# Layer-norm statistics of the output blocks taken by two accumulating passes on ScalarE in place of bn_stats on VectorE

## The reference, cut to what matters

```python
# x: (8, 2048, 1024) f32; 8 routed experts, top 2 of them weighted, and one shared expert; I = 1408
x = x + _layernorm(local_attention(_layernorm(x), w1, w2, v))       # window of 16 tokens
x = x + _layernorm(moe(_layernorm(x), w_router, wg, wu, wd, wg_s, wu_s, wd_s))

def _layernorm(x, axis=-1, eps=1e-5):
    m = jnp.mean(x, axis=axis, keepdims=True)
    v = jnp.var(x, axis=axis, keepdims=True)
    return (x - m) / jnp.sqrt(v + eps)
```

## Time and profile before

| what | us |
|---|---|
| median of 3 runs | 3217.65 |
| the profiled execution, its time | 3216.99 |
| its span (slowest core, core 4) | 3215.3 |
| spans of the 8 cores | 3204.2 to 3215.3 |
| last block's addition into osc ends | 3212.3 |

### The profile page before, as it was taken

How to read it: one execution, slowest core, us unless ns; L and a number is a source line. 1 busy time by engine, 2 the same in 40 slices (tenths; PEclk the granted TensorE clock), 3 DMA queues, 4 the chain that set the end, 5 groups by cost and what they waited for, 6 DMA issues and landing times.

```text
span 3215.3 us, 31801 instructions; the slowest of 8 cores (3204.2 to 3215.3 us)
## 1 busy us (share of the span) xinstructions
PE 2517.7 (78%) x11570; PEld 1123.4 (35%) x11570; DVE 1210.1 (38%) x2366; ACT 527.0 (16%) x474; POOL 506.6 (16%) x550
## 2 busy tenths in 40 slices
PE   2654554542128999999999999689999999999995
PEld 0221121210013444444444444334444444444442
DVE  5564655656543222222222222532222222222225
ACT  2422517061211011001001001010010010010010
POOL 0000000000002122222222222122222222222220
PEclk9986877766558999999999999799999999999997
DMA  7000000000206679669679777577787778878773
GB/s 165 1 0 1 1 1 1 1 0 0 20 1 64 63 66 91 62 64 91 66 66 85 71 74 72 81 79 67 65 86 72 71 74 75 76 66 79 75 65 73
DMA packets 626055, 179.41 MB, mean 56 GB/s; under 512 B 618608, under 2 KB 619760, under 8 KB 625904
## 3 DMA queue, kind: packets, MB, share of 16 engines
q0 software_dynamic: 621344, 160.55, 53.2%
q1 hardware_dynamic: 4560, 16.84, 1.5%
HBM read 329.48 MB, written 8.39 MB: 105 GB/s over the span
## 4 chain that ended last, share of the span: by engine, by line
PE 71%; DVE 14%; ACT 8%; issue 3%; DMA 2%; DVEq 2%; ACTq 0%; SPq 0%; POOLq 0%
PE py L944 21%; PE pg L856 12%; PE pu L871 12%; PE py L871 10%; PE py L856 10%; ACT tanb L394 6%; DVE uwide L470 3%; PE pq L320 2%; PE pq L339 1%; DVEq L62 1%; DVE bnb L154 1%; DVE argb L388 1%; DMA x<-x 1%; PE psc L403 1%; DMA wdb<-wd 1%
## 5 line engine op out<-in xcount | busy, mean ns | idle before, releaser
L944 PE MATMUL py<-hpr,wdb 128*128 128x512 bf16 x3168 | 706.3, 385 | 48.2 <-DVE hpr L893 40.0
L944 PEld LDWEIGHTS py<-hpr,wdb 128*128 128x128 bf16 x3168 | 312.0, 99 | 436.3 <-issue 81.0
L856 PE MATMUL pg<-xm_fm,wgb 128*128 128x512 bf16 x1728 | 394.9, 382 | 3.0 <-DVE cwb L811 3.0
L871 PE MATMUL pu<-xm_fm,wub 128*128 128x512 bf16 x1728 | 390.6, 379 | 0.0
L842 POOL DMA_DIRECT2D wgb<-wg x176 | 156.4, 889 | 1455.4 <-DVE x L577 812.3
L962 DVE SCALAR_TENSOR_TENSOR yfm<-py,yfm 128x1024 f32<-128x1024 f32 x128 | 156.8, 1225 | 487.3 <-PE py L944 480.3
L885 DVE TENSOR_TENSOR t1b<-sgb,pu 128x1024 bf16<-128x1024 bf16 x108 | 131.9, 1221 | 527.0 <-PE pu L871 527.0
L871 PE MATMUL py<-xm_fm,wub 128*128 128x512 bf16 x1440 | 325.5, 379 | 0.0
L856 PE MATMUL py<-xm_fm,wgb 128*128 128x512 bf16 x1440 | 325.5, 379 | 0.0
L881 ACT ACTIVATE sgb<-pg 128x1024 bf16<-128x1024 f32 x108 | 110.6, 1024 | 1297.6 <-PE pg L856 1297.6
L403 PE MATMUL psc<-tanb,vspb 128*16 128x512 bf16 x512 | 154.6, 431 | 188.6 <-ACT tanb L394 188.5
(11 more groups left out here) (119 smaller groups left out, 1308.6 us busy)
## 6 DMA issues: line engine op xcount, KB each, us to landing
wgb<-wg POOLq DMA_DIRECT2D x176, 256.0 KB, 5.2
wub<-wu POOLq DMA_DIRECT2D x176, 256.0 KB, 5.4
wdb<-wd POOLq DMA_DIRECT2D x128, 352.0 KB, 6.8
x<-x SPq DMA_DIRECT2D x4, 2048.0 KB, 27.7
out<-osc SPq DMA_DIRECT2D x16, 512.0 KB, 2.6
wgb<-wgs POOLq DMA_DIRECT2D x22, 256.0 KB, 5.3
wub<-wus POOLq DMA_DIRECT2D x22, 256.0 KB, 5.8
wdb<-wds POOLq DMA_DIRECT2D x16, 352.0 KB, 6.6
```

Of the source, the lines that this page charges most:

```text
L856: last = e.matmul(gb[:, gg * 512:(gg + 1) * 512], wgb[sl][:, c * 128:(c + 1) * 128], xm_fm[:, c * T + tof + gg * 512: c * T + tof + (gg + ...
L871: last = e.matmul(ub[:, gg * 512:(gg + 1) * 512], wub[sl][:, c * 128:(c + 1) * 128], xm_fm[:, c * T + tof + gg * 512: c * T + tof + (gg + ...
L944: last = e.matmul(pbank[pyn][:, gg * 512:(gg + 1) * 512], wdb[sl][:, ic * 128:(ic + 1) * 128], hpr[:, ic * TH + gg * 512: ic * TH + (gg + ...
```

## The change

The `bn_stats` and `bn_aggr` instructions of the epilogue go. In their place ACT reads the PSUM tile twice: an Identity activation that writes the block to `ytv` and accumulates the sum over the row, and a Square activation that writes to `osc` (the result is overwritten later in the same block) and accumulates the sum of squares. Four small DVE instructions make the mean and the variance of these two sums. The normalisation (L1015 before, L1027 after) reads `ytv` and no longer PSUM. The PSUM tile is given back to PE by the Square pass. The wait for `ytv_chain` moves from the normalisation on DVE to the Identity pass on ACT, and the Square pass gets the wait for the output DMA of two blocks before.

```diff
-                    for gi in range((H + 511) // 512):
...
-                        P.add("vector", lambda e, gi=gi, s0_=s0_, wdt=wdt, ob=ob,
-                              blk=blk: e.bn_stats(
...
-                    P.add("vector", lambda e, po=po, blk=blk: e.bn_aggr(
-                        agg2[:, po: po + 2],
-                        bnb[:, (blk % 2) * 12: (blk % 2) * 12 + 6 * nst]))
+                    zi = blk % 2
+                    evs1 = P.add("scalar", lambda e, ob=ob, zi=zi, po=po:
+                                 e.activation(
+                        ytv[zi][:], ob[:, 0:H], AF.Identity,
+                        accum_out=agg2[:, po: po + 1]),
+                        waits=[ev_yt, ytv_chain[0]], inc="s")
+                    evs2 = P.add("scalar", lambda e, ob=ob, zi=zi, po=po:
+                                 e.activation(
+                        osc[zi][:], ob[:, 0:H], AF.Square,
+                        accum_out=agg2[:, po + 1: po + 2]),
+                        waits=[evs1] + ev_out_dma[-2:-1], inc="s")
+                    free_ev[obk] = evs2
+                    P.add("vector", lambda e, po=po: e.tensor_scalar(
+                        agg2[:, po: po + 1], agg2[:, po: po + 1], 1.0 / H, None,
+                        op0=A.mult), waits=[evs2])
+                    P.drain("vector")
+                    P.add("vector", lambda e, po=po: e.tensor_scalar(
+                        agg2[:, po + 2: po + 3], agg2[:, po: po + 1],
+                        agg2[:, po: po + 1], None, op0=A.mult))
+                    P.drain("vector")
+                    P.add("vector", lambda e, po=po: e.tensor_scalar(
+                        agg2[:, po + 1: po + 2], agg2[:, po + 1: po + 2], 1.0 / H,
+                        None, op0=A.mult))
+                    P.drain("vector")
+                    P.add("vector", lambda e, po=po: e.tensor_tensor(
+                        agg2[:, po + 2: po + 3], agg2[:, po + 1: po + 2],
+                        agg2[:, po + 2: po + 3], op=A.subtract))
                     P.drain("vector")
                     evv = P.add("vector", lambda e, po=po: e.tensor_scalar(
-                        agg2[:, po + 2: po + 3], agg2[:, po + 1: po + 2], EPS,
+                        agg2[:, po + 2: po + 3], agg2[:, po + 2: po + 3], EPS,
                         None, op0=A.add), inc="v")
...
-                    evz = P.add("vector", lambda e, zi=zi, po=po, ob=ob:
-                                e.tensor_scalar(
-                        ytv[zi][:], ob[:, 0:H], agg2[:, po: po + 1],
+                    evz = P.add("vector", lambda e, zi=zi, po=po: e.tensor_scalar(
+                        ytv[zi][:], ytv[zi][:], agg2[:, po: po + 1],
                         agg2[:, po + 3: po + 4], op0=A.subtract, op1=A.mult),
-                        waits=[ev_a4, ytv_chain[0]], inc="v")
-                    free_ev[obk] = evz
+                        waits=[ev_a4], inc="v")
```

More of the change, by code:

```diff
@@ L987, in build_program @@
                     po = 4 * (blk % 2)
-                    for gi in range((H + 511) // 512):
-                        s0_ = gi * 512
-                        wdt = min(512, H - s0_)
-                        P.add("vector", lambda e, gi=gi, s0_=s0_, wdt=wdt, ob=ob,
-                              blk=blk: e.bn_stats(
[L993 to L997, removed]
@@ L1012, in build_program @@
                     P.drain("vector")
-                    zi = blk % 2
-                    evz = P.add("vector", lambda e, zi=zi, po=po, ob=ob:
-                                e.tensor_scalar(
-                        ytv[zi][:], ob[:, 0:H], agg2[:, po: po + 1],
+                    evz = P.add("vector", lambda e, zi=zi, po=po: e.tensor_scalar(
+                        ytv[zi][:], ytv[zi][:], agg2[:, po: po + 1],
                         agg2[:, po + 3: po + 4], op0=A.subtract, op1=A.mult),
-                        waits=[ev_a4, ytv_chain[0]], inc="v")
-                    free_ev[obk] = evz
+                        waits=[ev_a4], inc="v")
                     P.drain("vector")
```

## The result

The changed kernel takes 3235.42 us in the median, against 3218.21 for the kernel before measured beside it: the ratio is 1.0058, with a 95% interval of 1.004 to 1.0077. A second set of runs gave 1.0045 (1.0027 to 1.0063). It is a little slower, by about 16 us. The rows after come from the profile of the second set (span 3231.7 us on core 3, against 3215.3 before).

The account below looks back on a forecast made before the run. DVE was taken to bound the two epilogues, 16 blocks without overlap. Each block grows from 5.67 to 6.69 us, adding 16.3 us to the profiled 3216.99; with 0.66 for the median, 3234.0 us, range 3226 to 3249.

Parts of the forecast that it names:

- Steps 1 to 5: Epilogue block, from the addition's end: hand-overs between DVE and ACT plus Identity and Square passes, together 2.54 us.
- step 3: Between the ACT passes: Square waits for Identity's semaphore, taken as a hand-over of 0.10 us.
- step 4: Square pass on ACT: 1.12 us, its wait for the output DMA of two blocks before costing nothing.
- Rival B: ACT passes dearer than SiLU's row: 3240.5 us, or 3261 if accumulating takes two steps per element; chance 0.06.
- Step 6: Five small one-column DVE instructions between Square and the square root: 1.25 us per block.
- Step 7: Square root and reciprocal until the normalisation starts: 0.63 us per block, as before.
- Step 8: Normalisation on DVE, reading SBUF instead of PSUM: 0.81 us, against 1.344 before.
- Rival A: Normalisation gains nothing from SBUF and stays at 1.344 us: 3242.5 us in all; chance 0.10.
- Step 9: Gap and addition into osc at the block's end: 0.23 + 1.225 us, as before.
- Rival C: Activation table loads before Square and again before the root in every block: 38.7 us, 3272.7 us; chance 0.04.
- Rival D: ACT passes overlap DVE's work on the previous block: 4.25 us a block, 3194.9 us in all; chance 0.02.
- the cover: Outside the epilogue blocks: everything else stays as it is; a longer pause does not lower PE's clock for the second half.

Follow-up runs that it names:

- e10: Changed kernel with Square's unused result written to a dead tile instead of osc, without the output-DMA wait: ratio 1.0049.
- e5: Changed kernel with the normalisation reading the PSUM tile again, the Identity pass still writing ytv: ratio 1.0072.
- e3: Kernel before with two ytv buffers and an Identity copy to ytv on ACT, bn_stats and normalisation reading ytv from SBUF: 3211.08 us, ratio 0.9973.
- e1: Changed kernel with two ytv buffers, Identity waiting for the addition of two blocks before: 3200.47 us, ratio 0.995.
- e7: Changed kernel with three ytv buffers, two small DVE instructions for five, normalisation and addition behind the next block's small instructions: 3233.26 us, ratio 1.0031.
- e9: e7 with Square's unused result written to a dead tile, without the output-DMA wait: 3191.53 us, ratio 0.992.
- e11: Changed kernel with two ytv buffers, Square into a dead tile, one small DVE instruction before the root: ratio 0.9908, profiled execution 3189.24 us.

## Why the prediction was right

The forecast was 3234.0 us, the result 3235.42 (3232.71 in the second set), inside the range and on the side forecast. The steps, against the rows after:

- Steps 1 to 5, the turns and passes, 2.54 us: from the addition's end (3208.60, 3207.37 and 1.23) to the first small instruction (3211.17) are 2.57. Both passes have SiLU's 1.024 us as taken; the accumulator read takes 0.194 and adds 0.10. Square starts 1.26 us behind Identity where 1.22 was forecast (step 3's hand-over of 0.10 held); 0.05 of that is the wait for the DMA, which step 4 had priced at nothing (e10). Rival B, dearer passes, did not occur.
- Step 6, five small instructions, 1.25 us: 1.24 (3211.17 to 3212.41).
- Step 7, 0.63 us: 0.63 (3212.41 to 3213.04).
- Step 8, the normalisation, 0.81 us: 0.812. The number was right, its working was weaker than it reads: two rows of bf16 copies cannot give both a fixed part and a factor, and the 0.16 of step 8 comes out only if the doubling is put in. e5 and e3 show both ways that the gain goes with the source (or with working in place, see e5). By the Trainium skill ("VectorE: DVE Perf Modes", the perf-mode tier table) f32 tensor_scalar has a doubled rate in SBUF and the single one from PSUM; 0.812 and 1.344 us agree with both halves. Rival A is out.
- Step 9 stood. The sum is 6.71 against 6.69 us.
- Rival C, table loads: two loads at the root as before, none in front of Square. The 2.66 us of the Trainium skill ("ScalarE: Activation LUTs", What ACT_TABLE_LOAD costs) is not seen at this place: the load takes 1283 ns and the root follows at once. What Square would cost between two sets without it could not be tried here.
- Rival D, overlap, was excluded because of the one ytv; e1 shows that this was the only thing in the way. Its price for such a case, 4.25 us a block and 3194.9 us, came close to what e1 measured, 4.30 and 3200.5; the time differs more than the period since the passes of each half's first block stay exposed, and the gap of 0.16 behind the addition had been counted as 0.10.
- The first block of each half stands outside the seven periods. From the end of the last transpose into `pg` to the first addition are 5.60 us before and 6.64 after in the first half, 5.67 and 6.76 in the second. The second half, before and then after:

```profile
3165.12 0.30 PE L981 MATMUL pg<-idf,yfm 128*128 128x128 f32 x1 [0.72 <-DVE yfm L962]
...
3171.09 1.23 DVE L1021 TENSOR_TENSOR osc<-ytv,x 128x1024 f32<-128x1024 f32 x1 [0.23 <-DVE ytv L1015]
```

```profile
3173.12 0.30 PE L981 MATMUL pg<-idf,yfm 128*128 128x128 f32 x1 [0.72 <-DVE yfm L962]
...
3180.18 1.23 DVE L1032 TENSOR_TENSOR osc<-ytv,x 128x1024 f32<-128x1024 f32 x1 [0.23 <-DVE ytv L1027]
```

  With the 14 periods (7.0 and 7.3 us) the 16 blocks grew by 16.4 us, where 16.3 were forecast.
- Outside the epilogues, the cover held. From the last addition of the first half to the first matmul of the second are 1.63 us before and 1.74 after on most cores. The matmuls of the second half up to its epilogue take 1064.7 to 1065.5 us on the eight cores before and 1064.1 to 1066.7 after, so the longer pause at the low clock adds nothing that shows. Most cores are even some 0.5 us quicker there than before, in e1 too; why stays open.

What the prediction did not see is a second thing that Square hangs on: its throw-away output binds it to the output DMA. It cost 0.05 us a block here, and some 42 us in e7 (3233.26 against 3191.53 in e9). Step 4 reasoned that the landing is "more than a whole block earlier", which is true only while blocks are slow: with periods of 4.30 us (e1) it already holds Square up, for 2.6 us in 11 waits that DVE's work covers.

## What to carry to other kernels

Before work is moved to an engine that looks idle, follow the guards of the buffers that it will write: with one buffer the two engines take turns and the moved work stands on the path at full price (the kernel is 16 us slower here), with two it is hidden (17 us quicker than the kernel before). An output that nobody reads is still a write, and should go to a tile that nobody else is waiting for, least of all one that a DMA is emptying. And a change that bundles several edits is worth taking apart: here the source in SBUF was good for half a microsecond a block without the rest (e3, with two buffers), while the statistics on ACT paid only together with the second buffer.

## What the runs showed of the hardware

ACT and DVE did not slow each other on tiles of 128x1024 f32, ACT reading PSUM and writing SBUF, DVE reading and writing SBUF: in e1 and e11 the passes stay at 1.00 to 1.03 us, the normalisation at 0.81 and the addition at 1.23 while they run side by side. An Identity pass that stands behind the root and need not wait starts 0.1 us before the root has ended (in e1 the root lasts from 3173.91 to 3174.11, the pass starts at 3174.02), so ACT instructions overlap a little. One more wait in front of an ACT instruction costs 0.05 us even when it has long been fulfilled (1.26 against 1.20 to 1.21 us). And the cores of one run fall into two groups some 9 us apart, 3219 to 3223 and 3228 to 3232 us in the changed kernel, both of them moved by 15 to 17 us against the kernel before; the distance is there before the first epilogue (its first addition at 2044.6 to 2049.1 and 2051.1 to 2057.1), and its cause was not looked for.
